# Cross attention of six layers, products on four row groups at once instead of two

## The reference

```python
for i in range(6):
    xn = _adaln(x, noise_emb, n1_w[i], n1_b[i])          # layer norm, scale and shift
    q, k, v = jnp.split(xn @ qkv_w[i].T, 3, axis=-1)
    q, k, v = _rope(q.reshape(B, L, H, HD)), _rope(k.reshape(B, L, H, HD)), v.reshape(B, L, H, HD)
    x = x + _attn(q, k, v, src_mask).reshape(B, L, D) @ so_w[i].T
    xn = _adaln(x, noise_emb, n2_w[i], n2_b[i])
    q = _rope((xn @ cq_w[i].T).reshape(B, L, H, HD))
    k = _rope((context @ ck_w[i].T).reshape(B, LC, H, HD))
    v = (context @ cv_w[i].T).reshape(B, LC, H, HD)
    x = x + _attn(q, k, v, ctx_mask).reshape(B, L, D) @ co_w[i].T
    xn = _adaln(x, noise_emb, n3_w[i], n3_b[i])
    h = jax.nn.gelu(xn @ f1_w[i].T + f1_b[i], approximate=False)
    x = x + (h @ f2_w[i].T + f2_b[i])
```

## Time and profile before

| | |
|---|---|
| median of 3 runs | 2892.53 us |
| the profiled execution, its own time | 2894.29 us |
| its span, first to last instruction | 2892.5 us |
| its mean granted TensorE clock | 0.856 of full speed |
| stage C, first NORM1 to last FEED_BACK | 1106.2 to 2635.7 us |
| a layer in the steady state (NORM1 of unit 8 to that of unit 10) | 249.2 us |

### The profile page before, as it was taken

One profiled execution on the slowest core, in us unless ns is written; L12 is line 12 of the kernel. 1 busy time (PEld: TensorE's weight loads), 2 busy tenths in 40 slices (PEclk: granted clock), 3 DMA queues, 4 the chain that ended last, 5 costly groups with the idle time before them and its releaser, 6 DMA issues. The chain is left out here.

```text
span 2892.5 us, 32350 instructions
## 1 busy us (share of the span) xinstructions
PE 2426.3 (84%) x11288; PEld 956.9 (33%) x11288; DVE 1662.8 (57%) x3709; ACT 1171.5 (40%) x1984; POOL 148.1 (5%) x143
## 2 busy tenths in 40 slices
PE   5999788789996974888888989889798888874799
PEld 2333243433332651233223233222322323222244
DVE  4666758346565576764674574576458347622544
ACT  2333232112222332563655466365456537622121
...
PEclk9999988679997896896888699598879859955899
...
GB/s 131 1 1 0 1 1 0 103 1 1 1 1 1 1 43 44 23 1 22 39 1 23 1 39 1 22 39 1 23 1 39 1 22 23 1 0 91 0 1 8
DMA packets 38098, 54.35 MB, mean 19 GB/s; under 512 B 5137, under 2 KB 34610, under 8 KB 36402
## 3 DMA queue, kind: packets, MB, share of 16 engines
...
...
## 5 line engine op out<-in xcount | busy, mean ns | idle before, releaser
L2175 DVE TENSOR_REDUCE C_nm<-ps 128x1 f32<-128x512 f32 x768 | 501.0, 685 | 260.0 <-PE ps L1675 257.6
L2034 ACT ACTIVATE C_prob<-ps 128x512 f32<-128x512 f32 x768 | 430.2, 594 | 198.7 <-PE ps L1695 193.7
L1675 PE MATMUL ps<-C_ks,C_qs 62*128 62x512 bf16 x768 | 275.3, 439 | 52.7 <-DVE C_nm L2175 34.4
L1695 PE MATMUL ps<-C_qs,C_ks 64*128 64x512 bf16 x768 | 256.8, 408 | 43.3 <-ACT C_prob L2034 40.0
L1710 PE MATMUL ps<-C_prob,C_va 128*32 128x512 f32 x1536 | 218.4, 642 | 6.3 <-ACT C_prob L2034 6.3
L2127 ACT ACTIVATE C_u<-ps,C_biasx 77x512 f32<-77x512 f32 x192 | 120.8, 678 | 162.2 <-PE ps L1818 161.8
L1814 PE MATMUL ps<-C_qx,C_kc 32*77 32x512 f32 x384 | 160.6, 922 | 15.2 <-ACT C_u L2127 11.2
L1675 PEld LDWEIGHTS ps<-C_ks,C_qs 62*128 62x128 bf16 x768 | 59.8, 96 | 273.0 <-DVE C_nm L2175 173.0
L714 DVE TENSOR_REDUCE A_nm<-ps 128x2 f32<-128x1024 f32 x64 | 77.6, 1212 | 112.5 <-PE ps L497 112.4
L1695 PEld LDWEIGHTS ps<-C_qs,C_ks 64*128 64x128 bf16 x768 | 56.7, 94 | 255.8 <-ACT C_prob L2034 182.2
L1791 PE MATMUL ps<-C_kc,C_qx 32*128 32x308 f32 x384 | 98.8, 593 | 31.4 <-DVE C_nmx L2266 13.7
...
## 6 DMA issues: line engine op xcount, KB each, us to landing
...
D_w<-in_D_ew SPq DMA_DIRECT2D x8, 768.0 KB, 11.4
...
```

The lines of the kernel that those rows point to most:

```text
L1675: pe.matmul(ps[:, S_BANK + hp, :], lhsT=qs[side(hp, MAX_ROW), b, 2 * q + pq, t * P:(t + 1) * P], rhs=ks[side(hp, MAX_ROW), b, 2 * q + pq, ...
L1695: pe.matmul(ps[:, ST_BANK + hp, :], lhsT=ks[side(1 - hp, HALF), b, 2 * q + pq, kt * P:(kt + 1) * P], rhs=qs[side(1 - hp, HALF), b, 2 * q + ...
L2034: act.activation(prob[:, kt % 2, pq, 1 - hp, :], ps[:, ST_BANK + hp, :], ACT.Exp, scale=SCALE)\
L2175: dve.tensor_reduce(nm[:, q % 2, t, pq, hp:hp + 1], ps[:, S_BANK + hp, :], AX.X, ALU.max, negate=True).then_inc(max_done, 1)
```

## The change

1. A step of `MAX_X` has four products, one on each row group, and there are 4 steps instead of 8. The first two go to banks 0 and 1 (those of `S`), the other two to the next two of the ring. VectorE reduces the four banks in one go.
2. A step of `ST_X` has four products on the four row groups, in banks 2 and 3 (those of `ST`) and two of the ring; ScalarE exponentiates four banks in one go. The heads are laid out anew so that one step is one `WEIGH_X` (`headx`, `probx`).
3. `S` and `ST` count their banks by the same `filled` and `emptied` semaphores as the ring, in a common `take`.
4. The norm's product moves from ScalarE to VectorE: four `tensor_scalar` (subtract, multiply) per norm; the `lnu` step goes.
5. All tables are written anew. `WINDOW` goes from 1155 to 1214. Instructions are as many as before but for points 1 to 4. In one layer of the steady state, of steps on TensorE between these events, before and after (unit e even, o odd):

| from, to | S | ST | WEIGH | TURN_BACK, CONTEXT, OUT |
|---|---|---|---|---|
| MAX_X to TURN_MAX_X of o | 7, 5 | 0, 0 | 0, 0 | 0, 0 |
| TURN_MAX_X to OUT_X of o | 23, 23 | 9, 6 | 1, 1 | 0, 0 |
| OUT_X of o to NORM1 of o+2 | 20, 20 | 19, 25 | 5, 6 | 1, 1 |
| NORM1 of o+2 to MAX_X of e | 52, 54 | 54, 52 | 14, 13 | 5, 6 |
| MAX_X to TURN_MAX_X of e | 12, 5 | 14, 13 | 4, 4 | 2, 0 |
| TURN_MAX_X to OUT_X of e | 14, 21 | 19, 25 | 4, 5 | 1, 2 |
| OUT_X of e to NORM1 of e+2 | 0, 0 | 13, 7 | 4, 3 | 3, 3 |

```diff
+                def take(key, bank):
+                    uses[bank] += 1
+                    place[key] = bank, uses[bank]
+                    if uses[bank] > 1:
+                        pe.wait_ge(emptied[bank], uses[bank] - 1)
+                    return bank
...
-                def cross_max(c, i):
-                    t, gp = divmod(i, 2)
+                def cross_max(c, t):
...
-                    banks = [fill(("sx", c, i, gh)) for gh in range(2)]
-                    for gh in range(2):
-                        rows = slice(32 * (2 * gp + gh), 32 * (2 * gp + gh) + 32)
+                    banks = [take(("sx", c, t, r), S_BANK + r) for r in range(2)]
+                    banks += [fill(("sx", c, t, r)) for r in range(2, 4)]
+                    for r in range(4):
+                        rows = slice(32 * r, 32 * r + 32)
...
-                def cross_T(c, i):
-                    gp, j = divmod(i, 4)
+                def cross_T(c, q):
...
-                    banks = [fill(("stx", c, i, gh)) for gh in range(2)]
+                    banks = [take(("stx", c, q, r), ST_BANK + r) for r in range(2)]
+                    banks += [fill(("stx", c, q, r)) for r in range(2, 4)]
...
-                    for i in hits(at["EXP_X"], s):
-                        q, jj = divmod(i, 2)
+                    for q in hits(at["EXP_X"], s):
...
-                        for gh in range(2):
-                            bank = arrived(act, ("stx", n, i, gh))
-                            act.activation(probx[:, q % 2, jj, gh, :], ps[0:CTX, bank, :], ACT.Exp,
+                        for r in range(4):
+                            bank = arrived(act, ("stx", n, q, r))
+                            act.activation(probx[:, q % 2, r, :], ps[0:CTX, bank, :], ACT.Exp,
...
-                    dve.scalar_tensor_tensor(m.lnu[:, 0:TB], m.mv[:, 0:TB, 0], -1.0, m.rs[:, 0:TB], ALU.mult, ALU.mult)\
-                        .then_inc(seeded, 1)
+
+                def apply(n, count):
+                    for t in range(TB):
+                        k = n % B * TB + t
+                        ins = dve.tensor_scalar(m.xn[:, k, :], m.y[:, k, :], m.mv[:, t, 0:1], m.rs[:, t:t + 1],
+                                                ALU.subtract, ALU.mult)
+                        if t < TB - 1:
+                            c_.step(ins)
+                    ins.then_inc(xn_ready, 1)
...
-                    for i in hits(at["MAX_X"], s):
-                        t, gp = divmod(i, 2)
-                        for gh in range(2):
-                            bank = arrived(dve, ("sx", n, i, gh))
-                            dve.tensor_reduce(nmx[:, t, 8 * gp + 4 * gh:8 * gp + 4 * gh + 4],
+                    for t in hits(at["MAX_X"], s):
+                        for r in range(4):
+                            bank = arrived(dve, ("sx", n, t, r))
+                            dve.tensor_reduce(nmx[:, t, 4 * r:4 * r + 4],
```

More of the change, by code:

```diff
@@ L1330 @@
 GROUPS = TILES // 2
-WINDOW = 1155
+WINDOW = 1214
 TENSOR = (
[4 rows of a table removed]
-     "TURN_MAX": [755, 1009, 1234, 1441],
[4 rows of a table removed]
[L1344 to L1359, removed]
[8 rows of a table removed]
-     "TURN_MAX": [450, 625, 880, 1078],
[4 rows of a table removed]
[L1373 to L1392, removed]
[4 rows of a table added]
+     "TURN_MAX": [859, 1080, 1316, 1520],
[4 rows of a table added]
+     "WEIGH": [957, 999, 1032, 1061, 1221, 1253, 1286, 1370, 1423, 1474, 1506, 1541, 1604, 1637, 1669, 1704],
+     "TURN_BACK": [1087, 1401, 1561, 1724],
+     "CONTEXT": [1741],
+     "OUT": [1760],
+     "NORM2": [1858],
+     "CQ": [1878, 1887],
+     "MAX_X": [1935, 1974, 2007, 2047],
+     "TURN_MAX_X": [2092],
+     "ST_X": [2105, 2141, 2200, 2379],
+     "WEIGH_X": [2152, 2187, 2244, 2422],
+     "TURN_BACK_X": [2215, 2232, 2265, 2448],
+     "CONTEXT_X": [2477],
+     "OUT_X": [2494],
+     "NORM3": [2577],
+     "FEED": [2596, 2611, 2628, 2646],
+     "FEED_BACK": [2679],
[8 rows of a table added]
+     "TURN_MAX": [469, 655, 965, 1145],
[4 rows of a table added]
+     "WEIGH": [559, 599, 631, 686, 745, 783, 824, 861, 1067, 1100, 1132, 1177, 1251, 1292, 1325, 1354],
+     "TURN_BACK": [706, 882, 1219, 1374],
+     "CONTEXT": [1391],
+     "OUT": [1424],
+     "NORM2": [1658],
+     "CQ": [1678, 1687],
+     "MAX_X": [1718, 1744, 1770, 1824],
+     "TURN_MAX_X": [1877],
+     "ST_X": [1898, 1950, 2017, 2080],
+     "WEIGH_X": [1972, 2004, 2060, 2122],
+     "TURN_BACK_X": [2032, 2049, 2094, 2142],
+     "CONTEXT_X": [2160],
+     "OUT_X": [2180],
+     "NORM3": [2287],
+     "FEED": [2307, 2319, 2331, 2343],
+     "FEED_BACK": [2377],
+     "NORM1": [87],
+     "Q": [106, 118],
+     "K": [130, 142],
+     "V": [172]},
@@ L1393 @@
 )
 VECTOR = (
-    {"MAX": [537, 554, 570, 587, 603, 617, 625, 634, 647, 655, 669, 677, 700, 708, 730, 738, 757, 765, 773,
[3 rows of a table removed]
[L1399 to L1414, removed]
-     "ROTATE_Q": [388, 395],
-     "ADD_Q": [416],
-     "ROTATE_K": [402, 409],
-     "REST_Q": [434],
-     "LAST_Q": [455]},
@@ new lines @@
+    {"MAX": [289, 297, 308, 316, 324, 332, 342, 350, 364, 372, 380, 388, 406, 414, 422, 440, 452, 460, 471,
+             479, 487, 495, 505, 513, 527, 535, 543, 551, 565, 591, 623, 642, 653, 661, 670, 692, 706, 714,
+             752, 823, 863, 877, 885, 899, 908, 916, 924, 932, 954, 962, 970, 978, 988, 1003, 1017, 1025, 1038,
+             1048, 1056, 1069, 1082, 1090, 1098, 1117],
+     "SPLIT_MAX": [448, 650, 940, 1125],
+     "NORMALISE": [721, 892, 1228, 1383],
+     "OUT": [1435],
+     "STATS2": [1570],
+     "SEED2": [1590],
+     "ROTATE_X": [1694, 1701],
+     "ADD_X": [1709],
+     "MAX_X": [1728, 1754, 1788, 1842],
+     "SPLIT_MAX_X": [1869],
+     "NORMALISE_X": [2041, 2066, 2104, 2153],
+     "OUT_X": [2192],
+     "STATS3": [2206],
+     "SEED3": [2232],
+     "FEED_BACK": [2414],
+     "STATS1": [0],
+     "SEED1": [26],
+     "ROTATE_Q": [117, 131],
+     "ADD_Q": [172],
+     "ROTATE_K": [145, 159],
+     "REST_Q": [188],
+     "LAST_Q": [240],
+     "APPLY1": [59],
+     "APPLY2": [1622],
+     "APPLY3": [2264]},
@@ L1660, in _ @@
             def _(pe):
-                def fill(key):
-                    turn, i = divmod(len(place), len(RING))
-                    place[key] = bank, use = RING[i], turn + 1
-                    if use > 1:
-                        pe.wait_ge(emptied[bank], use - 1)
-                    return bank
+                uses, turns = dict.fromkeys(filled, 0), []
+                def take(key, bank):
[4 more added lines that the diff above has]
+                    return bank
+                def fill(key):
+                    turns.append(key)
+                    return take(key, RING[(len(turns) - 1) % len(RING)])
                 def scores(n, i, hp):
@@ L2215, in step @@
                         seed()
+                    if s in at["APPLY1"]:
+                        apply(n, norms(n, 0))
+                    if s in at["APPLY2"]:
+                        apply(n, norms(n, 1))
+                    if s in at["APPLY3"]:
+                        apply(n, norms(n, 2))
                     for k in hits(at["ROTATE_Q"], s):
@@ L2269, in step @@
                     if s in at["SPLIT_MAX_X"]:
-                        for k in range(16):
-                            drained(dve, ("sx", n, k // 2, k % 2))
+                        drained(dve, ("sx", n, TB - 1, 3))
                         if n:
```

267 lines of the change are left out of this document (123 added, 144 removed), and 58 rows, old and new, of tables (SCALAR, TENSOR, VECTOR).

## The result

The changed kernel takes 2794.16 us (median of 4 runs; the kernel before 2890.65 beside it), a ratio of 0.9669 with a 95% interval of 0.9624 to 0.9714. The forecast was 2804. The profiled execution went from 2894.29 to 2795.14 us, 99.2 less. 5.3 of these lie ahead of stage C, in stages whose code is the same.

The account below looks back on a forecast made before the run. Cross attention was taken as TensorE-bound, the odd unit's mostly at 1.2 GHz. Five periods gave -72.5 us, unit 0 -3.5, unit 11 -12: -88 on 2894.3, 2806, less 1.8 for the median: 2804; range 2760 to 2895.

Parts of the forecast that it names:

- the first period: From unit 0's NORM1 to unit 2's; unit 0's even cross attention was to gain 3.5 us.
- Odd MAX_X: Odd unit, MAX_X to TURN_MAX_X: 17.8 to 14.5 us, steps paced by VectorE's reductions, MAX_X3 also by maxima of S.
- Odd TURN_MAX_X to OUT_X: Odd unit's ST_X stretch: 44.4 to 37.2 us, less TensorE work, 2.5 us of new waits, clock left low.
- rival B: Denser steps raise the clock in the odd unit's ST_X stretch: 9 us more a layer, 2760 us; chance 0.13.
- Even MAX_X: Even unit, MAX_X to TURN_MAX_X: 16.9 to 14.0 us, TensorE and VectorE each waiting at times for the other.
- Even TURN_MAX_X to OUT_X: Even unit's ST_X stretch: cheaper steps against steps moved in, -0.4 us at the higher clock level, 0.6 gained at 0.72.
- Window 4: Odd unit's OUT_X to its NORM1: 2.2 us more TensorE work, two shorter norms, so +1.0 us on 29.1.
- Window 5: Dense self attention, 57.8 us: same work within 0.5 us, VectorE 1.0 more, so no change.
- The norm product: Moved to VectorE: each norm 0.7 us shorter on the path, 1.0 us more VectorE; bounds -0.7 to +1.0 each.
- D: Rival: in cross steps the four products run two by two, costing two pairs; no change, 2895 us; chance 0.06.
- A: Rival: draining four banks in a burst bounds cross steps, S and ST wait, clock falls; 2935 us; chance 0.14.
- C: Rival: only the odd unit gains, even units and moved steps lose to VectorE waits; 2848 us; chance 0.17.

Follow-up runs that it names:

- pairs-in-turn kernel: The changed kernel with the two pairs of products in each cross step issued one after the other; 2798.21 us, 0.9700 of the kernel before.

## Why the prediction was right, and where it was not

The time was right, and partly by luck, because misses offset each other. Worked by its own parts: the first period -3.5 forecast and +13.6 measured (+17.1 off); four layers -58.0 and -79.2 (-21.2 off); from unit 10's NORM1 to the end -26.5 and -28.6 (-2.1); and 5.3 us ahead of stage C, which no step foresaw.

- **The price of a step of four: right.** 2.37 and 1.24 us for the 2.5 and 1.35 forecast, MAX_X 1.67 at the lower level (1801.62 to the end of its bfloat16 part) for 1.7. The float32 part of four takes 1955.25 - 1954.33 = 0.92 us, of two 0.90, and not the 1.17 that I had estimated from the Trainium skill (TensorE: Matmul & The Clock Gate, Measured speedup vs the span model: 3.07 times for four row tiles). That estimate is not borne out; four against one, which the page measured, no run here shows.
- **Odd MAX_X: right,** 14.0 for 14.5, steps 3.05 apart for 3.2. The reasons, three reductions and then two maxima of S, stand.
- **Odd TURN_MAX_X to OUT_X: a term mis-sized, -13.3 for -7.2.** The step that failed is "I leave the clock at the lower level". It was 0.76. Four in the old order gave 36.7 at 0.60, with the norm product on VectorE 32.8 at 0.74, four in the new order 31.1 at 0.76, the same products on two groups 44.5 at 0.53: rival B's mechanism in half its size. It is the largest miss: over the four layers the window gained 55.4 us where 28.8 were forecast.
- **Even MAX_X: right in size,** 14.1 for 14.0, though not by the waits that I gave. TensorE's sum is 11.76; I wrote 11.4, where my own terms give 10.8 (16.4 - 3.0 - 2.6). Of the 2.3 us in which it stands idle, 1.8 are waits for ScalarE's exponentials and 0.4 for VectorE. The old-order run shows what the term rested on without my saying so: without the seven S moved out, the stretch grows to 20.1 or more.
- **Even TURN_MAX_X to OUT_X: -5.2 for -0.6 in the layer of the table, from two errors that work against each other.** "-0.4 at the higher level" failed: at clock 1.00 on both sides, in unit 0, the stretch went from 31.0 to 36.9 us (rows below). TensorE's part grew by 2.2, its idle time by 3.7, with ScalarE busy 27 us in it instead of 24. The steps of four saved 8 x 1.24 - 4 x 1.24 = 5.0 there, so those moved in took about 7.2 and not the 4.1 that I put on them. The other error is the clock, which I had kept at 0.72: it is 1.00 after, and in units 6 and 8 that gave back more than the loss. In unit 4 it did not (35.8 to 38.0), and units 0 and 10, at 1.00 already before, lost 5.9 each.
- **Window 4: +3.0 for +1.0.** TensorE has 3.0 us more in it (25.0 to 28.0), where I had counted 2.2 and let the shorter norms cover half.
- **Window 5: +2 to +4 for 0.** At clock 1.00 it takes 60.0 us where ST_X alone was on two groups and 59.8 where MAX_X was in the ring, so some 2 us are not clock. VectorE's added norm product is not enough for them: alone it gave 58.0. Four in the old order gave 59.3 with the norm product on ScalarE, so sharing the banks of S and ST may be most of it; no run parts this from the new order. The rest is clock: after had 0.94 and 61.9, the pairs-in-turn kernel 0.87 and 65.0 in the same layer.
- **The norm product: the weakest step.** The shorter chain and VectorE's microsecond per norm were each as I said (341 ns, 40.0 us for 144), and yet their net was taken as one number. It is +0.9% or -2.3%, by the order around it.
- **Unit 11's cross attention: -16.4 for -12.** 57.4 to 41.0 us: MAX_X takes 12.1 for my 12.8, but behind it the clock is 0.68 where I had kept 0.50. That covers the rest of the last part, which came short: -12.2 for -14.5.
- **The first period: not foreseen.** Three windows of it, before and then after, are S31 to S63, S63 to ST63, and unit 0's TURN_MAX_X to OUT_X:

```profile
1159.80:1205.20 45.40, 38.70 (x180) 11.54 (x176) 35.06 (x90) 25.47 (x49) 3.90 (x3) 0.85 0.11 30
1205.20:1223.30 18.10, 14.23 (x93) 3.91 (x90) 13.04 (x26) 12.10 (x23) 0.00 (x0) 1.00 0.06 17
1262.60:1293.60 31.00, 28.84 (x184) 9.04 (x181) 13.08 (x30) 23.86 (x44) 0.00 (x0) 1.00 0.01 2
```
```profile
1155.80:1206.40 50.60, 44.69 (x179) 12.70 (x176) 36.28 (x92) 23.83 (x45) 3.58 (x3) 0.76 0.08 21
1206.40:1229.60 23.20, 18.81 (x95) 4.55 (x92) 13.60 (x26) 12.43 (x23) 0.00 (x0) 0.78 0.09 25
1266.80:1303.70 36.90, 31.03 (x207) 9.52 (x206) 18.25 (x39) 27.09 (x50) 0.00 (x0) 1.00 0.01 2
```

The same work takes 5.2 and 5.1 us longer at a lower clock, before any cross product has run. The first of these windows takes 45.3 us in both kernels of the old order that were cut in the same way (four products alone, norm product alone), and 53.1 and 53.3 in two more of the new order (pairs in turn, norm product back): it is the order that brings it, whichever engine has the norm product. Why the clock is lower in that order stays open.

Of the rivals, D (two by two) is out by 1.24 us a step. A, the drain that bounds, did not decide after, but it is real in the old-order kernel's window 6. The Trainium skill (TensorEngine Tiling (Array Packing), PSUM Bottleneck: tiling speeds TensorE and not the emptying of PSUM) agrees with that run: TensorE's part fell from 16.4 to 13.6 us, VectorE's stayed (14.6 and 14.4), and the window grew to 20.1. A's price has a slip: 29 us of work at 1.0 are 58 at 0.5 and not near 50, so the window would lose 16 us and not 8. B, a higher clock in the odd unit, came true by half, as said. C, a gain in the odd unit that is lost elsewhere, is what four in the old order did, down to no gain at all. In after, its sign was there (window 5 above 60 us in three of the four layers) and its price was not.
